# Query rows of the later attentions: written straight into the query buffer, with repeats copied inside it, in place of a round trip through DRAM

## The chip, the cores and the metric

The kernel runs on one core of a Trainium2 chip. Its time is the device time of one execution in microseconds (us). The core has five engines: TensorE (PE, matrix products, with PEld for its weight loads), VectorE (DVE), ScalarE (ACT), GpSimd (POOL) and SyncE (SP), which here does nothing but issue transfers. Sixteen DMA engines move the data; all transfers that SP issues go through one queue (q1 in the profile), those that ACT issues through another (q10).

## The reference

Eight batches of 256 rows with 256 columns go through a chain of eight residual blocks: an attention with 16 heads, a choice of one expert out of eight, a masked attention with 16 heads, a small coupling network, a linear attention, a top-2 mixture with low-rank experts, an attention with one head, and a gated feed-forward block. The change concerns the two 16-head attentions:

```python
q = proj(Q, W_Q, b_Q)                      # (B, 16 heads, 256, 16)
k = proj(K, W_K, b_K)
scores = jnp.einsum('bhqd,bhkd->bhqk', q, k) / jnp.sqrt(jnp.float32(D_K))
attn = jax.nn.softmax(scores, axis=-1)     # the second one: masked first
out = jnp.einsum('bhqk,bhkd->bhqd', attn, v)
x = x + _L0_xattn_ref(_layernorm(x, axis=-1), ctx_1024, ctx_1024, ...)
```

## The kernel before

**Attentions.** There are 16 of them, `(b, m)` with batch `b` and `m` 0 or 1, in the order (0,0), (1,0), (0,1), (2,0), (1,1), (3,0), (2,1) and so on to (7,0), (6,1), (7,1). The scores are formed in bf16, but from numbers that were split into three bf16 parts each, so that the product is as good as one in float32. A head has 16 dimensions, and six products of parts are summed in one matmul over 96 rows: the query buffer `QA[m]` has six blocks of 16 partitions, block `i` being rows 16i to 16i+15, and on each row 16 heads x 256 positions (8 KB). Blocks 0, 1 and 2 hold part 0 of the query, blocks 3 and 4 part 1, block 5 part 2. The key buffer `KA[m]` has the partner parts in its blocks. Two more rows of `QA[m]`, 96 and 97, hold the negative row maximum in two bf16 parts.

**How a query gets there.** A projection on PE leaves the query with (dimension, head) on the partitions; ACT and POOL split it into `qparts[m]` (128 partitions x 2 halves x 3 parts x 256). `QA[m]` wants the dimension alone on the partitions, and the heads along the row. Before the change the two halves of `qparts[m]` are written to a DRAM tensor, `scratch` (line 466, two transfers of 192 KB), and when both have landed, read back block by block (line 499, six transfers of 128 KB). The keys take the same way (lines 466 and 481) and go on doing so. Only the very first attention (0,0) is fed straight from `qparts[0]` and `kparts`: 12 transfers of 64 KB for each of the two, issued by SP (line 521) and ACT (line 785).

**Two passes over the scores.** `heads(b, m)` (line 1586) forms all scores once, so that DVE can take the maximum of each row. For each group of four heads PE turns the maxima (line 1653), ACT copies them into `negm` (line 843), and SP sends them into rows 96 and 97 of `QA[m]`: two transfers of 2 KB a group (line 559). Then the scores are formed once more, transposed and with the maximum subtracted by these two rows (line 1674); the first matmul of each group waits for its two transfers (`m_rows`). From there they go to ACT for the exponential (line 855), back to PE for the sum over values (line 1696), and so on.

**What sets the order.** Every engine runs its instructions strictly in the order in which the program was written. Six threads (`p` preparation, `s` scores, `v` the second pass and what follows, `a`, `b`, `c` the later blocks) are interleaved by one string of letters for each engine, `TURNS`; a letter lets that thread go on to its next `yield`. SP's queue is therefore one list in which the transfers of all threads stand, and a wait in it holds back everything behind it:

```python
def weave(engine, prep, score, value, net, rest, last, early=iter(()), late=iter(())):
    threads = {"p": prep, "s": score, "v": value, "a": net, "b": rest, "c": last, "w": early, "z": late}
    for who in TURNS[engine]:
        next(threads[who], None)
```

Queries of `m` = 0 are fed by the thread `p`, a batch or more ahead of their use; those of `m` = 1 by the thread `s`, one attention ahead. PE's list also holds matmuls on a blank tile, at the beginning and at the end (line 1967).

Of the kernel before, what the change touches and what calls it, by code (L numbers as in the profile page):

```python
# [16 lines left out]
KT = D // P  # L17
H, HD = 16, 16
GH = 4
ITEMS = H // GH  # L20
PARTS = 6

GROUPS = [(0, 3), (1, 2), (2, 1)]
# [110 lines left out]
PLACE = {bm: q for q, bm in enumerate(ATTENTIONS)}  # L134
# [40 lines left out]
def program(nc, x_in, ctx_in, mask_in, pack, nomask, ipack, scratch, out):  # L175
    ctx = ExitStack()
    with ctx:
# [5 lines left out]
        def sem(name, n=0):  # L183
            s = ctx.enter_context(nc.semaphore(name))
            per[s.name] = n
            return s

        def nth(s, r, n):
            return r * per[s.name] + n
# [36 lines left out]
        qparts = [sb(f"qparts{m}", [P, KT, 3, S], BF16) for m in range(2)]  # L226
        KA = [sb(f"KA{m}", [KM, H, S], BF16) for m in range(2)]
        QA = [sb(f"QA{m}", [KM, H, S], BF16) for m in range(2)]
# [88 lines left out]
        for who, steps in LAST.items():  # L317
            done = 0
            for i, name in enumerate(steps):
                n = steps[:i + 1].count(name)  # L320
# [35 lines left out]
        k_ps, v_ps, q_ps = ([sem(f"{n}{m}", 1) for m in range(2)] for n in ("k_ps", "v_ps", "q_ps"))  # L356
        k_f, q_f, v_s = ([sem(f"{n}{m}", 1) for m in range(2)] for n in ("k_f", "q_f", "v_s"))
        k_split, q_split = ([sem(f"{n}{m}", 1) for m in range(2)] for n in ("k_split", "q_split"))
        k_out, q_out = ([sem(f"{n}{m}", 16 * KT) for m in range(2)] for n in ("k_out", "q_out"))
        k_rows = [sem(f"k_rows{m}", 16 * len(GROUPS)) for m in range(2)]  # L360
        q_rows = [sem(f"q_rows{m}", 16 * PARTS) for m in range(2)]
        q_part, q_first, k_first = sem("q_part"), sem("q_first"), sem("k_first")
        third_pe, third_act, third_dve = sem("third_pe", 5), sem("third_act", 3), sem("third_dve", 4)
        xb0_s, xe_s, xb1_s = sem("xb0", 1), sem("xe", 1), sem("xb1", 1)
# [4 lines left out]
        st_ps, exp_s = sem("st_ps"), sem("exp_s")  # L369
# [39 lines left out]
        for name, n in (("sc", E + E * R), ("tw", E * R), ("r1", E), ("r2", E), ("r3", E), ("pick2", E),  # L409
# [9 lines left out]
            s={**{name: last_did[who] for name, who in WHO.items()}, "m_in_s": last_mask_in}, **small_at)  # L419
# [13 lines left out]
        def q_cut(eng, m, b):  # L433
            if (m, b) == (0, 0):
                eng.wait_ge(q_part, 3)
            else:
                eng.wait_ge(q_split[m], nth(q_split[m], b - (m == 0), 1))

        def q_sent(eng, m, b):
            if (m, b) == (0, 0):  # L440
                eng.wait_ge(q_first, 16 * KT * PARTS)
            else:
                eng.wait_ge(q_out[m], nth(q_out[m], b - (m == 0), 16 * KT))

        def q_landed(eng, m, b):
            if (m, b) == (0, 0):
                eng.wait_ge(q_first, 16 * KT * PARTS)
            else:
                eng.wait_ge(q_rows[m], nth(q_rows[m], b - (m == 0), 16 * PARTS))

        block = ctx.enter_context(nc.Block())

# [4 lines left out]
        def _(sp):  # L457
# [6 lines left out]
            def write(parts, which, m, out_s):  # L464
                for k in range(KT):
                    sp.dma_start(scratch[m, which, :, k * P:(k + 1) * P, :].rearrange("c p s -> p c s"),
                                 parts[:, k, :, :]).then_inc(out_s[m], 16)
# [16 lines left out]
                    yield  # L484

            def queries(b, m):
                if b:
                    q_landed(sp, m, b - 1)
                q_cut(sp, m, b)
                write(qparts[m], 0, m, q_out)  # L490
                yield
                q_sent(sp, m, b)
                if b:
                    sp.wait_ge(st_ps, (PLACE[b - 1, m] + 1) * H)
                at = 0
                for part, n in GROUPS:
                    src = scratch[m, 0, part].rearrange("(d h) s -> d (h s)", h=H)
                    for i in range(at, at + n):
                        sp.dma_start(QA[m][i * HD:(i + 1) * HD, :, :].rearrange("p h s -> p (h s)"), src
                                     ).then_inc(q_rows[m], 16)  # L500
                        if i % 2:
                            yield
                    at += n

            def next_cin(b):
                if b < B:
# [1563 lines left out]
```

## Time and profile before

| what | value |
|---|---|
| median of 3 runs | 1091.88 us (1087.68 to 1097.86) |
| the profiled execution, its own time | 1095.82 us |
| its span, first to last instruction | 1094.0 us |
| PE, DVE, ACT, POOL busy | 94%, 59%, 47%, 20% |
| mean granted TensorE clock | 0.975 of full speed |
| DMA: bytes moved, mean rate | 57.07 MB, 52 GB/s |

The profile is that of one execution. Busy time is the union of an engine's instructions; the span is what lies between the first and the last of them, and 1.8 us of the execution's own time lie outside it.

### The profile page before, as it was taken

What the parts mean: (1) busy time and instruction counts of PE and PEld (TensorE: products, weight loads), DVE (VectorE), ACT (ScalarE), POOL (GpSimd) and SP (SyncE); (2) the same over time, 40 slices, a digit from 0 to 9 for tenths busy, and PEclk for the clock granted to TensorE, in tenths of its full rate; (3) what the DMA queues carried; (4) which work ended last, traced back from release to release, by engine and by line L of the source; (5) the groups of instructions that cost most, each with busy time, mean ns of one, the idle gap of its engine ahead of it and who ended that gap; (6) DMA issues with size and microseconds to landing.
All of it is one profiled execution on the core that took longest, in us unless ns stands there. A gap on an engine that the chain in (4) does not pass through costs nothing.

```text
span 1094.0 us, 17887 instructions
## 1 busy us (share of the span) xinstructions
PE 1027.3 (94%) x6322; PEld 700.0 (64%) x6322; DVE 646.5 (59%) x2246; ACT 510.1 (47%) x1091; POOL 220.6 (20%) x314
## 2 busy tenths in 40 slices
PE   7699999888999999999999999999999999999988
PEld 5365664555567765767576756776666756667767
DVE  4245673657667565666667565766667555535553
ACT  1050543465247542574247533574366343765311
POOL 2021330214030220313030222213121112001200
PEclk9599999989999999999999999999999999999999
DMA  7426630324022220403121230412041003000000
GB/s 230 47 52 185 174 83 6 63 45 88 21 47 52 53 46 20 97 10 78 30 57 42 54 63 2 98 43 56 1 86 27 11 7 75 4 10 1 1 10 11
DMA packets 43175, 57.07 MB, mean 52 GB/s; under 512 B 4488, under 2 KB 39056, under 8 KB 39568
## 3 DMA queue, kind: packets, MB, share of 16 engines
q1 hardware_dynamic: 40880, 47.16, 20.1%
q10 hardware_dynamic: 2208, 8.78, 2.6%
q8 instruction: 51, 0.84, 0.3%
q14 instruction: 36, 0.29, 0.1%
HBM read 40.19 MB, written 13.89 MB: 49 GB/s over the span
## 4 chain that ended last, share of the span: by engine, by line
PE 79%; ACT 7%; DMA 4%; DVE 4%; issue 3%; SPq 1%; POOL 1%; ACTq 0%; DVEq 0%
PE bank L1614 11%; PE bank L1947 7%; PE bank L1465 6%; PE bank L1474 6%; PE bank L1674 5%; PE bank L1696 5%; PE bank L1958 4%; PE bank L1731 4%; PE bank L1586 4%; PE bank L1967 3%; DMA QA<-negm 2%; PE bank L1725 2%; PE bank L1677 2%; PE bank L1483 2%; PE bank L1908 1%
## 5 line engine op out<-in xcount | busy, mean ns | idle before, releaser
L855 ACT ACTIVATE PT<-bank 128x512 f32<-128x512 f32 x256 | 153.0, 598 | 194.4 <-PE bank L1677 131.2
L1614 PE MATMUL bank<-w,xhT 128*128 128x512 f32 x256 | 129.0, 610 | 0.0
L1674 PE MATMUL bank<-QA,KA 98*128 98x256 bf16 x512 | 116.1, 280 | 10.7 <-ACT PT L855 7.4
L1153 DVE CUSTOM_DVE_ANT_0 bank<-bank,maskb 128x256 f32<-128x256 f32 x256 | 102.3, 451 | 33.5 <-PE bank L1586 33.1
L1146 DVE TENSOR_REDUCE mx<-bank 128x2 f32<-128x512 f32 x128 | 83.7, 683 | 39.8 <-PE bank L1586 39.3
L1586 PE MATMUL bank<-KA,QA 96*128 96x256 bf16 x512 | 90.9, 279 | 12.6 <-DMA QA<-qparts 8.9
L1198 DVE SCALAR_TENSOR_TENSOR x<-bank,one,x 128x256 f32<-128x256 f32 x128 | 61.8, 483 | 61.1 <-PE bank L1614 58.4
L1947 PE MATMUL bank<-xhBT,wi 128*128 128x256 f32 x336 | 86.7, 391 | 5.2 <-DVE hT L1450 5.1
L1674 PEld LDWEIGHTS bank<-QA,KA 98*128 98x128 bf16 x512 | 46.0, 100 | 68.0 <-ACT PT L855 36.9
L1696 PE MATMUL bank<-PT,vaug 128*32 128x256 f32 x1024 | 72.7, 393 | 3.0 <-ACT PT L855 3.0
L1586 PEld LDWEIGHTS bank<-KA,QA 96*128 96x128 bf16 x512 | 45.7, 100 | 39.3 <-issue 14.8
L1947 PEld LDWEIGHTS bank<-xhBT,wi 128*128 128x128 f32 x336 | 59.8, 192 | 16.9 <-DVE hT L1450 7.4
L1967 PE MATMUL bank<-blank 128*128 128x256 bf16 x440 | 66.8, 289 | 1.2 <-POOL blank L715 1.1
L1677 PE MATMUL bank<-maskb,identb 128*128 128x256 bf16 x256 | 64.9, 277 | 0.0
L1614 PEld LDWEIGHTS bank<-w,xhT 128*128 128x128 f32 x256 | 42.7, 193 | 26.7 <-issue 22.3
L1967 PEld LDWEIGHTS bank<-blank 128*128 128x128 bf16 x440 | 43.6, 103 | 13.4 <-issue 4.8
L1731 PE MATMUL bank<-xhAT,w 128*128 128x256 f32 (+1 forms) x216 | 49.8, 364 | 1.6 <-ACT xhAT L887 1.2
L622 POOL TENSOR_TENSOR kparts<-kf,kparts 128x512 bf16<-128x512 f32 x16 | 18.5, 1157 | 159.3 <-ACT kf L747 159.3
L855 ACT ACT_TABLE_LOAD x36 | 46.2, 1283 | 0.6
L1696 PEld LDWEIGHTS bank<-PT,vaug 128*32 128x32 f32 x1024 | 32.4, 110 | 19.0 <-ACT PT L855 5.9
L695 POOL TENSOR_TENSOR veps_b<-mv_b,epsm 128x2 f32<-128x2 f32 x21 | 4.1, 195 | 197.7 <-DVE mv_b L1333 197.7
L1958 PE MATMUL bank<-wi,hT 128*128 128x256 f32 x168 | 42.4, 385 | 0.0
(310 smaller groups left out, 2013.0 us busy)
## 6 DMA issues: line engine op xcount, KB each, us to landing
QA<-scratch SPq DMA_DIRECT2D x90, 128.0 KB, 4.3
scratch<-kparts SPq DMA_DIRECT2D x30, 192.0 KB, 2.3
KA<-scratch SPq DMA_DIRECT2D x15, 384.0 KB, 4.5
scratch<-qparts SPq DMA_DIRECT2D x30, 192.0 KB, 2.3
KA<-scratch SPq DMA_DIRECT2D x15, 256.0 KB, 5.2
wi<-ipack ACTq DMA_DIRECT2D x1, 2304.0 KB, 8.5
w<-pack ACTq DMA_DIRECT2D x1, 2169.0 KB, 14.5
xin<-x_in SPq DMA_DIRECT2D x8, 256.0 KB, 3.2
```

Source lines behind the costliest of these rows:

```text
L855: act.activation(PT[:, n % RING, :, :].rearrange("p t s -> p (t s)"), st_bank[:, :], ACT.Exp).then_inc(exp_s, 1)
L1146: dve.tensor_reduce(mx[:, i % 4, n % GH, :], s_bank[n % 2][:, :].rearrange("p (t s) -> p t s", t=T), AX.X, ALU.max).then_inc(max_s, 1)
L1153: last = dve.tensor_tensor_reduce(s, s, maskb[:, t, :], op0=ALU.add, op1=ALU.max, scale=1.0, scalar=-HUGE, accum_out=mx[:, i % 4, n % GH, ...
L1586: last = pe.matmul(s_bank[n % 2][:, t * S:(t + 1) * S], QA[m][0:KR, u, t * P:(t + 1) * P], KA[m][0:KR, u, :], start=True, stop=True)
L1614: last = pe.matmul(bank[n % 2][:, :], xhT[:, kk, t * P:(t + 1) * P], W("exp0", KT)[:, kk, i * 512:(i + 1) * 512], start=(kk == 0), stop=(k ...
L1674: last = pe.matmul(st_bank[:, t * S:(t + 1) * S], KA[m][0:KM, v, t * P:(t + 1) * P], QA[m][0:KM, v, :], start=True, stop=(m == 0))
L1677: last = pe.matmul(st_bank[:, t * S:(t + 1) * S], identb[:, :], maskb[:, t, :], start=False, stop=True)
L1696: last = pe.matmul(pv_bank[32 * h:32 * h + 32, 0:S], vaug[m][:, t, g * GH + h, :], PT[:, (i * GH + h) % RING, t, :], start=(t == 0), stop= ...
L1731: last = pe.matmul(ps[:, k * S + lo * P:k * S + hi * P], W(name, KT)[:, kk, k * P:(k + 1) * P], src[:, kk, lo * P:hi * P], start=(kk == 0) ...
L1947: last = pe.matmul(ps[:, i * S + lo * P:i * S + hi * P], ww[:, kk, k * P:(k + 1) * P], L.xhBT[:, kk, lo * P:hi * P], start=(kk == 0), stop ...
L1958: last = pe.matmul(ps[:, t * D:(t + 1) * D], hid[:, kk, t * P:(t + 1) * P], wd[:, kk, :], start=(kk == 0), stop=(kk == HT - 1))
L1967: pe.matmul(ps[:, 0:S], blank[:, 0:P], blank[:, :], start=True, stop=True)
```

## The change

The queries of every attention after (0,0) no longer pass through `scratch`. When the query is split and the buffer is free, SP sends each of the three parts once, straight from `qparts[m]` into blocks 0, 3 and 5 of `QA[m]`: two transfers of 64 KB a part, six in all, each into 8 partitions, with a semaphore `q_once`. When all six have landed, three transfers of 128 KB inside `QA[m]` copy block 0 to blocks 1 and 2 and block 3 to block 4 (`q_rows`). ACT's wait before it overwrites `qparts[m]` is now for `q_once`, and the first matmul of `heads` waits for both semaphores. The number of `yield`s is the same, so the turns of every engine fall as before. The wait for the last second-pass matmul of the attention that used the buffer before (`st_ps`) now stands ahead of the first transfers, and the wait for the old `q_rows` ahead of them is gone.

```diff
--- before.py
+++ after.py
@@ -356,9 +356,10 @@
         k_ps, v_ps, q_ps = ([sem(f"{n}{m}", 1) for m in range(2)] for n in ("k_ps", "v_ps", "q_ps"))
         k_f, q_f, v_s = ([sem(f"{n}{m}", 1) for m in range(2)] for n in ("k_f", "q_f", "v_s"))
         k_split, q_split = ([sem(f"{n}{m}", 1) for m in range(2)] for n in ("k_split", "q_split"))
-        k_out, q_out = ([sem(f"{n}{m}", 16 * KT) for m in range(2)] for n in ("k_out", "q_out"))
+        k_out = [sem(f"k_out{m}", 16 * KT) for m in range(2)]
+        q_once = [sem(f"q_once{m}", 16 * KT * 3) for m in range(2)]
         k_rows = [sem(f"k_rows{m}", 16 * len(GROUPS)) for m in range(2)]
-        q_rows = [sem(f"q_rows{m}", 16 * PARTS) for m in range(2)]
+        q_rows = [sem(f"q_rows{m}", 16 * 3) for m in range(2)]
         q_part, q_first, k_first = sem("q_part"), sem("q_first"), sem("k_first")
         third_pe, third_act, third_dve = sem("third_pe", 5), sem("third_act", 3), sem("third_dve", 4)
         xb0_s, xe_s, xb1_s = sem("xb0", 1), sem("xe", 1), sem("xb1", 1)
@@ -440,13 +441,14 @@
             if (m, b) == (0, 0):
                 eng.wait_ge(q_first, 16 * KT * PARTS)
             else:
-                eng.wait_ge(q_out[m], nth(q_out[m], b - (m == 0), 16 * KT))
+                eng.wait_ge(q_once[m], nth(q_once[m], b - (m == 0), 16 * KT * 3))
 
         def q_landed(eng, m, b):
             if (m, b) == (0, 0):
                 eng.wait_ge(q_first, 16 * KT * PARTS)
             else:
-                eng.wait_ge(q_rows[m], nth(q_rows[m], b - (m == 0), 16 * PARTS))
+                eng.wait_ge(q_once[m], nth(q_once[m], b - (m == 0), 16 * KT * 3))
+                eng.wait_ge(q_rows[m], nth(q_rows[m], b - (m == 0), 16 * 3))
 
         block = ctx.enter_context(nc.Block())
 
@@ -484,23 +486,19 @@
                     yield
 
             def queries(b, m):
-                if b:
-                    q_landed(sp, m, b - 1)
                 q_cut(sp, m, b)
-                write(qparts[m], 0, m, q_out)
-                yield
-                q_sent(sp, m, b)
                 if b:
                     sp.wait_ge(st_ps, (PLACE[b - 1, m] + 1) * H)
-                at = 0
-                for part, n in GROUPS:
-                    src = scratch[m, 0, part].rearrange("(d h) s -> d (h s)", h=H)
-                    for i in range(at, at + n):
-                        sp.dma_start(QA[m][i * HD:(i + 1) * HD, :, :].rearrange("p h s -> p (h s)"), src
-                                     ).then_inc(q_rows[m], 16)
-                        if i % 2:
-                            yield
-                    at += n
+                for part, i in ((0, 0), (1, 3), (2, 5)):
+                    for k in range(KT):
+                        sp.dma_start(QA[m][i * HD + k * 8:i * HD + (k + 1) * 8, :, :].rearrange("d h s -> d (h s)"),
+                                     qparts[m][:, k, part, :]).then_inc(q_once[m], 16)
+                yield
+                q_sent(sp, m, b)
+                for src, i in ((0, 1), (0, 2), (3, 4)):
+                    sp.dma_start(QA[m][i * HD:(i + 1) * HD, :, :].rearrange("p h s -> p (h s)"),
+                                 QA[m][src * HD:(src + 1) * HD, :, :].rearrange("p h s -> p (h s)")).then_inc(q_rows[m], 16)
+                    yield
 
             def next_cin(b):
                 if b < B:
```

SP's list in the steady part, where the queries of (b, 0) are fed while (b-1, 1) is in its second pass (so the maxima go to `QA1`). Before:

```order
L466 DMA scratch<-qparts0 128x3x256 [waits q_split0,q_rows0]
L466 DMA scratch<-qparts0 128x3x256
L559 DMA QA1<-negm 1x4x256 [waits negm_s]
L559 DMA QA1<-negm 1x4x256
L499 DMA QA0<-scratch 16x4096 [waits st_ps,q_out0]
L499 DMA QA0<-scratch 16x4096 x5
L559 DMA QA1<-negm 1x4x256 [waits negm_s]
```

The same place in SP's list with the change:

```order
L494 DMA QA0<-qparts0 8x16x256 [waits st_ps,q_split0]
L494 DMA QA0<-qparts0 8x16x256 x5
L557 DMA QA1<-negm 1x4x256 [waits negm_s]
L557 DMA QA1<-negm 1x4x256
L499 DMA QA0<-QA0 16x4096 [waits q_once0]
L499 DMA QA0<-QA0 16x4096 x2
L557 DMA QA1<-negm 1x4x256 [waits negm_s]
```

Ahead of the first pair of maxima stand six transfers where two stood, and ahead of the second pair three where six stood, behind another wait.

SP's list where the queries of (b, 1) are fed just before the first maxima of (b+1, 0) are due (these go to `QA0`). Before:

```order
L466 DMA scratch<-qparts1 128x3x256 [waits q_split1,q_rows1]
L466 DMA scratch<-qparts1 128x3x256
L499 DMA QA1<-scratch 16x4096 [waits st_ps,q_out1]
L499 DMA QA1<-scratch 16x4096 x3
L559 DMA QA0<-negm 1x4x256 [waits negm_s]
L559 DMA QA0<-negm 1x4x256
L499 DMA QA1<-scratch 16x4096 x2
```

The same place in SP's list with the change:

```order
L494 DMA QA1<-qparts1 8x16x256 [waits st_ps,q_split1]
L494 DMA QA1<-qparts1 8x16x256 x5
L499 DMA QA1<-QA1 16x4096 [waits q_once1]
L499 DMA QA1<-QA1 16x4096
L557 DMA QA0<-negm 1x4x256 [waits negm_s]
L557 DMA QA0<-negm 1x4x256
L499 DMA QA1<-QA1 16x4096
```

Here the pair of maxima stands behind eight transfers and the wait for `q_once1`, where it stood behind six and the wait for `q_out1`. On the other engines no instruction has moved.

## Rows read from the trace of the kernel before

**Rows 1.** The page: chain that ended last, shares of the span by engine.

```profile
PE 79%; ACT 7%; DMA 4%; DVE 4%; issue 3%; SPq 1%; POOL 1%; ACTq 0%; DVEq 0%
```

**Rows 2.** Busy time by stretch: stretch, us, then each engine; PEclk, DMA share, GB/s.

```profile
167.20:170.40 3.20, 3.14 (x9) 1.55 (x10) 0.12 (x1) 0.60 (x1) 0.00 (x0) 0.50 0.02 5
500.00:620.00 120.00, 116.92 (x719) 79.23 (x719) 76.59 (x272) 62.47 (x130) 27.24 (x37) 1.00 0.22 49
```

**Rows 3.** What PE waited for from 140 to 860 us: total, times, longest.

```profile
PE bank L1674 <- DMA QA<-negm: 2.5, 6, 1.2
```

**Rows 4.** The page, transfers by line: count, KB of each, median us to landing.

```profile
QA<-scratch SPq DMA_DIRECT2D x90, 128.0 KB, 4.3
...
scratch<-qparts SPq DMA_DIRECT2D x30, 192.0 KB, 2.3
```

**Rows 5.** Lines 499 and 521 alone: ns that SP takes to issue one; landing for line 499.

```profile
L499 SPq DMA_DIRECT2D QA<-scratch x90: 315/420/1629, 83.5 to 911.4; - x90
...
DMA to landing us min/median/max: 2.8/4.3/9.5
...
L521 SPq DMA_DIRECT2D QA<-qparts x12: 609/710/2088, 23.4 to 33.6; - x12
```

**Rows 6.** Busy time by stretch: straight copies at the start; scratch write, then block reads.

```profile
20.00:22.00 2.00, 2.00 (x21) 1.79 (x20) 0.00 (x0) 0.00 (x0) 2.00 (x3) 1.00 0.44 89
41.00:43.00 2.00, 0.00 (x0) 0.00 (x0) 0.00 (x0) 0.00 (x0) 0.00 (x0) 0.50 0.64 60
...
443.00:444.00 1.00, 1.00 (x8) 0.81 (x7) 0.96 (x5) 0.08 (x1) 0.00 (x0) 1.00 0.84 265
...
447.00:448.00 1.00, 1.00 (x10) 0.86 (x9) 0.22 (x1) 0.29 (x3) 1.00 (x2) 1.00 1.07 131
```

**Rows 7.** SP in order of time, 441 to 457 us: start, us, line.

```profile
441.61 0.90 SPq L466 DMA_DIRECT2D scratch<-qparts  x2
444.36 1.71 SPq L499 DMA_DIRECT2D QA<-scratch  x4
446.75 1.22 SPq L559 DMA_DIRECT2D QA<-negm  x2
448.02 1.02 SPq L499 DMA_DIRECT2D QA<-scratch  x2
```

**Rows 8.** The chain that ended last, 441 to 457 us: start, us, what.

```profile
447.40 3.75 DMA QA<-negm
...
451.19 0.39 PE bank L1674 x2
```

**Rows 9.** SP in order of time, 388.5 to 405 us.

```profile
389.48 0.91 SPq L466 DMA_DIRECT2D scratch<-qparts  x2
391.60 1.20 SPq L559 DMA_DIRECT2D QA<-negm  x2
```

**Rows 10.** PE in order of time, 388.5 to 405 us.

```profile
396.40 0.37 PE L1674 MATMUL bank<-QA,KA 98*128 98x256 bf16 x1
```

**Rows 11.** The chain that ended last, 262.5 to 272 us.

```profile
262.80 0.38 SPq L466
...
264.38 1.61 DMA QA<-negm
...
266.04 0.28 PE bank L1674
...
268.72 0.35 ACT negm L843
...
269.71 4.01 DMA QA<-negm
```

**Rows 12.** The last attention (7,1): SP, then PE, in order of time.

```profile
905.51 0.91 SPq L466 DMA_DIRECT2D scratch<-qparts  x2
908.27 4.25 SPq L499 DMA_DIRECT2D QA<-scratch  x6
...
917.26 0.60 PE L1586 MATMUL bank<-KA,QA 96*128 96x256 bf16 x4
```

More of the change, by code:

```diff
@@ L486, in queries @@
             def queries(b, m):
+                q_cut(sp, m, b)
                 if b:
-                    q_landed(sp, m, b - 1)
-                q_cut(sp, m, b)
-                write(qparts[m], 0, m, q_out)
+                    sp.wait_ge(st_ps, (PLACE[b - 1, m] + 1) * H)
+                for part, i in ((0, 0), (1, 3), (2, 5)):
+                    for k in range(KT):
+                        sp.dma_start(QA[m][i * HD + k * 8:i * HD + (k + 1) * 8, :, :].rearrange("d h s -> d (h s)"),
+                                     qparts[m][:, k, part, :]).then_inc(q_once[m], 16)
                 yield
                 q_sent(sp, m, b)
-                if b:
-                    sp.wait_ge(st_ps, (PLACE[b - 1, m] + 1) * H)
-                at = 0
-                for part, n in GROUPS:
-                    src = scratch[m, 0, part].rearrange("(d h) s -> d (h s)", h=H)
-                    for i in range(at, at + n):
-                        sp.dma_start(QA[m][i * HD:(i + 1) * HD, :, :].rearrange("p h s -> p (h s)"), src
-                                     ).then_inc(q_rows[m], 16)
-                        if i % 2:
-                            yield
-                    at += n
+                for src, i in ((0, 1), (0, 2), (3, 4)):
+                    sp.dma_start(QA[m][i * HD:(i + 1) * HD, :, :].rearrange("p h s -> p (h s)"),
+                                 QA[m][src * HD:(src + 1) * HD, :, :].rearrange("p h s -> p (h s)")).then_inc(q_rows[m], 16)
+                    yield
             def next_cin(b):
```

## The prediction

> **What bounds the kernel now.** First the chain that ended last, by engine: PE holds 79% of the span, and no other engine more than 7% [rows 1]. Then busy time by stretch: in the steady part, where one batch takes some 122 us, PE is busy 116.92 us of 120 [rows 2], so it stands still for 3 us a batch, and whatever makes it stand still longer goes nearly whole into the time. Its list is in one fixed order; it cannot go round a wait. So the question is which transfers PE waits for. The list of PE's waits names only one in the steady part: the first second-pass matmul of a group (line 1674) waits for the row maxima, `QA<-negm`, 2.5 us in 6 times [rows 3]. That sum is small, but the transfer stands on the chain with far more than the idle time: 3.75 us at 447.40 [rows 8], 1.61 and 4.01 us at 264.38 and 269.71 [rows 11]. It is 2 KB; it takes that long only because SP's list and queue put it behind the query blocks. The copy of the query itself is never waited for after the start: it lands well ahead of its `heads`, with one close case, the last [rows 12]. I therefore read the change by one thing: what it does to the maxima that stand behind the queries in SP's list. There are 15 such places ("visits"), one for each attention after (0,0).
>
> **Removed.** Two writes of 192 KB into the scratch, 2.3 us to land [rows 4], moving 265 GB/s [rows 6], and six block reads of 128 KB at 131 GB/s [rows 6], 1.0 us each when queued, with 0.42 us of SP each [rows 5]. None of it is waited for by itself; what it costs is the place it takes ahead of the maxima.
>
> **Added: six straight transfers of 64 KB.** The trace has twelve of the same shape, for (0,0), line 521. SP needs 0.71 us for one, against 0.45 for a scratch write (0.90 for two) [rows 5, 7]: six take 4.3 us of SP where the writes took 0.9. Their rate is the disputed number. At 20 to 22 us, where the issue set the pace, the same shape moved 89 GB/s; from 41 to 43 us, with a backlog, 60 GB/s with the DMA engines busy 0.64 and nothing else going on [rows 6]. The scratch write, with the same 512-byte pieces from the same tile, moved 265. So it is the destination, 8 partitions, that is slow: reads into 16 partitions moved 131 [rows 6], about twice as much. The bounds are: as fast as SP issues (4.3 us), or 60 GB/s. I take 60, since six are a backlog: 6 x 65.5 KB / 60 GB/s = 6.6 us. To that comes what the scratch write needs beyond its transfer, 2.3 - 197 KB / 265 GB/s = 1.5 us. The six have landed 8.1 us after the first issue, where the scratch write let SP go on 2.75 us after it (441.61 to 444.36) [rows 7].
>
> The Trainium skill ("SBUF — State Buffer", "Door 1: The DMA port swizzle") has a rule that speaks against this change: DMA bandwidth goes by how many of 16 ports the partitions reach, some 27 GB/s each. By its table 8 partitions in a row reach two ports, 54 GB/s, and 16 reach four, 109; the trace shows 60 and 131, in the same proportion. With 54 the six would take 7.3 us instead of 6.6, and the sum below would be 9 us higher.
>
> **Added: three copies inside `QA`.** No row shows one. The block reads write the same 16 partitions, 1.0 us each when queued, 2.8 us at least to land [rows 5, 6]. I take that, as the destination is the same. From below: without DRAM at the source, perhaps half a us less to land. From above: reading 16 partitions as slowly as 8 are written, 2.2 us each.
>
> **Visits where the maxima stand right behind the six** (all of m = 0 after (1,0), and those of (0,1) and (1,1): eight). At 389.48 SP issues until 393.8, where the maxima went out at 391.60 [rows 9]; they now lie behind the six in the queue and land at 389.5 + 8.1, PE goes on 0.3 us later, at 397.9. It used them at 396.40 [rows 10]: 1.5 us late. At 262.80 the same gives 271.2 against 266.04, 5.2 late; but the next pair then waits behind no copies. It was ready at 269.07 and took 4.6 us in all; ready at 274.3 it takes 0.6 + 1.6 (the unhindered landing at 264.38) and lands at 276.5 against 273.7, so 2.8 us of the 5.2 are left [rows 11]. The same arithmetic over the eight, from 116.26 to 753.93, gives 0.3, 2.5, 3.0, 2.8, 1.5, 1.8, 1.4 and 0: 13.3 us.
>
> **Visits where the maxima stand behind copies too** ((2,1), (3,1), (4,1), (5,1) behind two, (6,1) behind three). At 441.61: the six have landed at 449.7, where SP now waits with the maxima (ready since 446.75) behind it. Two copies 0.84, the pair 1.2 [rows 5, 7]; the first copy lands at 449.7 + 2.8 = 452.5, the second at 453.5, the maxima at 453.7. Before: 451.15 [rows 8]. 2.6 us late, on the chain. Four of these 10.4 us, (6,1) 1.7: 12.1 us.
>
> **The last one**, (7,1): the copies land at 905.51 + 8.1 + 2.8 + 2.0 = 918.4, PE wanted them at 917.26 [rows 12]: 1.3 us. The first, (1,0), is fed long before its use: nothing.
>
> **Edits with no cost.** `st_ps` ahead of the first transfer: its matmuls had ended before every visit, so SP does not wait there. ACT's wait for `q_once`: a batch old. PE's second wait: the same landing.
>
> **Sum.** 13.3 + 12.1 + 1.3 = 26.7 us of PE standing still. Not all of it stays: PE idles 3 us a batch anyway, and a stall lets ACT and DVE get ahead, so that some of that idle time goes. I take 0.8: 21 us. Against that, stalls cost clock. Right after the longest wait for maxima (1.2 us) the granted clock was 0.50 from 167.2 to 170.4 us, that is 1.2 GHz where 2.4 GHz is full [rows 2, 3]; 3.2 us at half speed cost up to 1.6 us. Fourteen new stalls might bring none, or one each (24 us); I take three, 5 us. So +26 us: the profiled execution would go from 1095.8 (span 1094.0) to 1122, and the median of the three runs, 1091.88, to **1118 us**, 2.4% slower. A measurement of this kernel can tell about 1% from no change.
>
> **The rivals.**
>
> *The straight transfers run at the pace of SP.* For it: 89 GB/s at 20 us [rows 6]; against it: the long stretch at 60. Six would land after about 6 us. The places behind copies come out even (441.61 + 6.1, copies and pair issued by 449.8, landed at 451), the places behind the six lose about 1 us each on average: +5 us, 1097 us, no change that can be told. This is the case that isn't slower. Chance 0.15.
>
> *Faster.* If SP also issued a straight transfer in 0.45 us, as it does a scratch write, the six would land after 4.5 us and the maxima at 441.61 would come 1.9 us sooner than now, since two copies stand ahead of them and not four. It decides at an issue below 0.55 us and a rate above 110 GB/s together. Five such visits and the pairs behind six copies give -12 us, 1080 us. Every one of the twelve issues took 0.609 us or more [rows 5]: 0.03.
>
> *Copies inside `QA` are slow.* At 2.2 us each the five visits behind copies lose 2.3 to 3.4 us more, and the second pairs of the early visits also: +16 before the factor, in all 39 us, 1131 us. No row excludes it: 0.14.
>
> *The clock goes with most stalls.* Ten dips and more: +38 us, 1130 to 1138 us: 0.08.
>
> **How the numbers follow.** The forecast has 0.60, with a range of its own from 1105 to 1128 (factor 0.5 to 1, none to five dips, 54 or 60 GB/s). The range that should hold 8 in 10 takes in the nearer half of the fast case and the slow copies: 1098 to 1134. Slower by over 1% (above 1103): 0.60 + 0.14 + 0.08 = 0.82; within 1%: 0.15; faster: 0.03.
>
> **What would show it.** In the list of waits, PE at the second-pass matmul for `QA<-negm` should grow from 2.5 us to over 20 in the same stretch. SP should wait for `QA<-qparts` 3 to 4 us at every visit. With one of the six in the queue behind another, the rate should be 60 GB/s. The copies should land one us apart. If the six land within 6 us, or PE's waits don't grow, the forecast is wrong; if the waits grow and the time doesn't, the factor is.

## The result: 5.2% slower, and the profile after

The changed kernel takes **1146.88 us** (median of four runs, 1145.75 to 1148.35) against 1093.22 us (1087.68 to 1097.86) for the kernel before: ratio 1.052, 95% interval 1.047 to 1.057. The forecast of 1118 had the direction and the place right, and about half of the size; the time is outside the range of 1098 to 1134. (A repetition, e0 below, gives the same; one of its four executions ran in a slower state of the chip, 1157.98 us at a clock of 0.945, and is left out.)

The pages: busy time before the change, then busy time and the chain that ended last by engine with it:

```profile
PE 1027.3 (94%) x6322; PEld 700.0 (64%) x6322; DVE 646.5 (59%) x2246; ACT 510.1 (47%) x1091; POOL 220.6 (20%) x314
```

```profile
PE 1047.0 (92%) x6322; PEld 711.0 (62%) x6322; DVE 646.8 (57%) x2246; ACT 510.7 (45%) x1091; POOL 220.4 (19%) x314
...
PE 67%; ACT 8%; DMA 7%; SPq 6%; POOL 4%; DVE 4%; issue 3%; ACTq 0%; DVEq 0%
```

Against [rows 1], SP's own issuing (SPq) went from 1% of the chain to 6% and DMA from 4% to 7%. PE does the same 6322 matmuls as before in 1047.0 us instead of 1027.3. The span is 1143.9 us instead of 1094.0. That closes the account: **+49.9 us is +30.2 us of PE idle (96.9 for 66.7) and +19.7 us of PE being busy longer with the same work.** The start hides a part of it. Counted from PE's first matmul of the first attention's `heads` (at 45.90 us before, 39.17 with the change), the rest takes 1048.1 and 1104.7 us for the same 6182 matmuls: +56.6 us, 33.9 of them idle and 22.7 busy.

What PE waited for (total, times, longest), from 140 to 900 us, the same places as in [rows 3], and then over the whole run:

```profile
PE bank L1672 <- DMA QA<-negm: 34.8, 11, 5.6
...
PE bank L1672 <- DMA QA<-negm: 36.1, 12, 5.6
...
PE bank L1584 <- DMA QA<-qparts: 4.2, 1, 4.2
```

The wait for the maxima went from 2.5 us in 6 to 34.8 us in 11; over the whole run it was 2.8, so it grew by 33.3. The last line is the start, where the kernel before waited 8.9 us; it happened to give 4.7 us back; e0, the same kernel again, doesn't wait there at all.

The two new lines of SP alone (ns to issue one: least, median, most), and what line 499's copies took to land and made wait:

```profile
L494 SPq DMA_DIRECT2D QA<-qparts x90: 608/609/1655, 70.7 to 960.1; - x90
...
L499 SPq DMA_DIRECT2D QA<-QA x45: 524/584/1726, 82.1 to 964.7; - x45
...
  PE bank L1584: 1.4, 1
...
DMA to landing us min/median/max: 3.3/3.8/12.7
```

The visit that answers to [rows 7, 8] (the one at 441.61 before), first SP in order of time, then the chain:

```profile
462.76 3.98 SPq L494 DMA_DIRECT2D QA<-qparts  x6
471.30 1.22 SPq L499 DMA_DIRECT2D QA<-QA  x2
472.56 1.69 SPq L557 DMA_DIRECT2D QA<-negm  x2
```

```profile
466.13 5.15 DMA QA<-qparts
...
471.30 0.59 SPq L499
...
471.93 0.58 SPq L499
...
472.56 0.66 SPq L557
...
473.26 2.64 DMA QA<-negm
...
475.94 0.39 PE bank L1672 x2
```

This is the cause at the five visits where the maxima stand behind copies, in six lines. SP issues six transfers until 466.7, then waits at its next instruction until they have landed, at 471.3; 8.5 us have gone by in which SP could send nothing else. Two copies follow, and only then the maxima, which had been ready since 467.9. They leave at 472.6 and land at 475.9.

At the eight visits where the maxima stand right behind the six, SP doesn't wait for a landing ahead of them. There they lose the 4 us of the six issues, and then are long in flight, since the six are still under way. The chain at the visit that answers to [rows 11], and at the same place in e4, where the six land faster:

```profile
271.57 3.99 DMA QA<-negm
```

```profile
266.68 1.68 DMA QA<-negm
```

PE in order of time at this visit and at the one before it in the text, with the wait ahead of the matmul in brackets:

```profile
275.61 0.39 PE L1672 MATMUL bank<-QA,KA 98*128 98x256 bf16 x1 [5.56 <-DMA QA<-negm]
...
475.94 0.39 PE L1672 MATMUL bank<-QA,KA 98*128 98x256 bf16 x2 [3.84 <-DMA QA<-negm]
```

Busy time by stretch, with PEclk, DMA share and GB/s at the end, as in [rows 2, 6]: the six in flight, the copies in flight, and the stretches at half clock by the two waits above:

```profile
466.00:467.00 1.00, 1.00 (x9) 0.92 (x8) 0.85 (x4) 1.00 (x4) 0.45 (x1) 1.00 0.63 62
472.00:473.00 1.00, 0.10 (x1) 0.00 (x0) 0.42 (x1) 0.84 (x2) 0.00 (x0) 1.00 1.06 123
476.40:483.00 6.60, 6.60 (x23) 4.59 (x21) 3.10 (x9) 1.32 (x4) 0.00 (x0) 0.50 0.33 102
271.50:281.60 10.10, 5.99 (x31) 2.54 (x32) 2.28 (x10) 1.90 (x4) 1.82 (x3) 0.50 0.41 53
```

The six move 62 GB/s, the copies 123, about as forecast. What was not forecast is the third and fourth row: with a standstill of 3.84 us the granted clock is at 0.50 (1.2 GHz) for the next 6.6 us, and around the one of 5.56 us for over 10 us, in 5.99 of which PE works. Half of the working time is lost: up to 3.3 and 3.0 us. Mean clock of the run, kernel before and changed kernel:

```profile
core 0: 1094.0 us, clock 0.975
```

```profile
core 0: 1143.9 us, clock 0.952
```

If all that is missing is time at 0.50, then 2 x (1 - clock) x span is the time spent at 1.2 GHz: 55 us before, 110 us after. Half of the 55 us more is lost work, up to 27 us, less where a part of it falls into a standstill; 19.7 showed.

### The profile page after: what moved, and what is told of

Its sections match the earlier page's. It is cut to its first block, busy times and chain, and to the rows that moved or that the text cites. A ratio compares the mean times of both kernels' runs of the same rounds, so it can differ in the third digit from the quotient of the medians.

```text
span 1143.9 us, 17895 instructions
## 1 busy us (share of the span) xinstructions
PE 1047.0 (92%) x6322; PEld 711.0 (62%) x6322; DVE 646.8 (57%) x2246; ACT 510.7 (45%) x1091; POOL 220.4 (19%) x314
## 4 chain that ended last, share of the span: by engine, by line
PE 67%; ACT 8%; DMA 7%; SPq 6%; POOL 4%; DVE 4%; issue 3%; ACTq 0%; DVEq 0%
PE bank L1612 10%; PE bank L1945 6%; PE bank L1672 5%; PE bank L1694 5%; PE bank L1463 4%; PE bank L1472 4%; SPq L494 4%; PE bank L1956 4%; DMA QA<-qparts 3%; DMA QA<-negm 3%; PE bank L1729 3%; PE bank L1584 3%; PE bank L1965 3%; PE bank L1675 2%; PE bank L1481 2%
## 5 line engine op out<-in xcount | busy, mean ns | idle before, releaser
L1672 PE MATMUL bank<-QA,KA 98*128 98x256 bf16 x512 | 119.9, 288 | 43.7 <-DMA QA<-negm 36.1
L1584 PE MATMUL bank<-KA,QA 96*128 96x256 bf16 x512 | 94.2, 288 | 8.7 <-DMA QA<-qparts 4.2
L1694 PEld LDWEIGHTS bank<-PT,vaug 128*32 128x32 f32 x1024 | 32.7, 111 | 18.8 <-ACT PT L853 5.5
```

Source lines behind the costliest of these rows:

```text
L1584: last = pe.matmul(s_bank[n % 2][:, t * S:(t + 1) * S], QA[m][0:KR, u, t * P:(t + 1) * P], KA[m][0:KR, u, :], start=True, stop=True)
L1672: last = pe.matmul(st_bank[:, t * S:(t + 1) * S], KA[m][0:KM, v, t * P:(t + 1) * P], QA[m][0:KM, v, :], start=True, stop=(m == 0))
L1694: last = pe.matmul(pv_bank[32 * h:32 * h + 32, 0:S], vaug[m][:, t, g * GH + h, :], PT[:, (i * GH + h) % RING, t, :], start=(t == 0), stop= ...
```

## The experiments

All twelve runs together. "Maxima" is PE's wait for `QA<-negm`; "idle" is span less PE busy; "at 1.2 GHz" is worked out as above. "Behind the start" is the span from PE's first matmul of the first attention's `heads` on. Those four are from the one profiled execution, the time is the median of the timed runs, and the ratio is against the kernel before on the same chip.

| run | us | ratio (95%) | maxima | idle | at 1.2 GHz | behind the start |
|---|---|---|---|---|---|---|
| kernel before | 1093.22 | | 2.8 | 67 | 55 | 1048 |
| changed kernel | 1146.88 | 1.052 (1.047, 1.057) | 36.1 | 97 | 110 | 1105 |
| e0, changed again | 1141.87 | 1.050 (1.042, 1.058) | 37.7 | 95 | 98 | 1104 |
| e1, maxima first | 1153.74 | 1.055 (1.047, 1.064) | 44.5 | 113 | 109 | 1112 |
| e2, scratch once | 1131.75 | 1.033 (1.025, 1.042) | 22.8 | 82 | 72 | 1084 |
| e3, PE given blank work | 1132.64 | 1.035 (1.027, 1.043) | 9.3 | 67 | 45 | 1086 |
| e4, rows apart | 1100.30 | 1.010 (1.006, 1.013) | 7.5 | 65 | 75 | 1065 |
| e7, order changed | 1113.51 | 1.022 (1.017, 1.027) | 8.2 | 82 | 58 | 1065 |
| e8, rows apart and order | 1080.89 | 0.993 (0.990, 0.996) | none listed | 59 | 35 | 1044 |
| e5, before with rows apart | 1080.12 | 0.993 (0.989, 0.997) | 0.6 | 55 | 45 | 1042 |
| e13, e5 again | 1081.62 | 0.989 (0.985, 0.993) | 0.9 | 57 | 30 | 1040 |
| e9, e5 with the order | 1092.32 | 0.999 (0.995, 1.002) | 4.3 | 65 | 50 | 1055 |
| e11, before, SP held | 1177.23 | 1.077 (1.071, 1.082) | 57.5 | 126 | 140 | 1137 |
| e12, ACT sends the maxima | 1134.27 | 1.039 (1.033, 1.045) | 11.3 | 100 | 85 | 1099 |

The start needs care. PE waits there for the queries of (0,0), which only the runs with rows apart feed differently: 8.8 to 9.7 us in the profiled executions of the kernel before, e1, e7, e11 and e12, 4.2 in that of the changed kernel, and nothing in the others, e0 among them. The first `heads` start at 44.9 to 45.9 us in the first group and at 34.6 to 36.2 in the last. So spans and idle times of single executions differ by some 10 us for this alone (that of e2 lay 11 us and that of e3 9 us under its median, that of e12 11 us above); the last column is free of it.

### e1: the maxima ahead of the six

The theory was that the maxima are late because they stand behind the six transfers. At 13 visits the next pair of maxima is moved ahead of them in SP's list.

```diff
+def maxima_first(turns):
+    at = {t: [i for i, c in enumerate(turns) if c == t] for t in "ps"}
+    visits = [at["p"][15 + 14 * (b - 2) + 8] for b in range(2, B)] + [at["s"][4 * b] for b in range(B - 1)]
...
+        turns[i:j + 1] = ["v"] + turns[i:j]
...
+TURNS["sync"] = maxima_first(TURNS["sync"])
```

> The changed kernel with one edit in SP's list: at 13 of the 15 visits the pair of maxima that stood next behind the six straight transfers goes ahead of them. Theory A (PE's standstill comes from maxima that stand behind the straight transfers in SP's list and in the queue, and all of the loss, the clock dips too, follows from that): PE's waits for QA<-negm fall from 36 us to under 8, the half-speed time after the start falls from about 90 us to about 30, and the time goes back to 1092 to 1105 us. Theory B (the straight transfers cost something by themselves, by contention with PE's reads of QA, or the queries come too late): the waits move to the heads (line 1584) or PE is slower everywhere, and the time stays above 1130 us.

It cured nothing: 1153.74 us, and the wait for maxima grew to 44.5 us. SP in order of time, and PE behind it:

```profile
479.94 1.22 SPq L571 DMA_DIRECT2D QA<-negm  x2
481.26 3.98 SPq L508 DMA_DIRECT2D QA<-qparts  x6
489.77 1.86 SPq L513 DMA_DIRECT2D QA<-QA  x3
491.67 1.16 SPq L596 DMA_DIRECT2D xhB<-ctx_in  x1
492.94 1.07 SPq L482 DMA_DIRECT2D scratch<-kparts  x2
494.05 1.32 SPq L571 DMA_DIRECT2D QA<-negm  x2
```

```profile
497.41 0.61 PE L1686 MATMUL bank<-QA,KA 98*128 98x256 bf16 x2 [5.25 <-DMA QA<-negm]
```

The pair moved ahead is in time; the **next** pair, ready at 488.5, now lies behind the landing, three copies and two further jobs, and PE stands 5.25 us for it. So the six transfers are not an obstacle for one pair: from the first of them to the landing SP's list is closed for 8.5 us, and whichever pair falls due meanwhile is late.

### e2: half of the change

One write to the scratch, three block reads, and the three repeats copied inside `QA`. This tells the straight transfers apart from the copies.

```diff
+                write(qparts[m], 0, m, q_out)
+                yield
+                sp.wait_ge(q_out[m], nth(q_out[m], b - (m == 0), 16 * KT))
...
-                    for k in range(KT):
-                        sp.dma_start(QA[m][i * HD + k * 8:i * HD + (k + 1) * 8, :, :].rearrange("d h s -> d (h s)"),
-                                     qparts[m][:, k, part, :]).then_inc(q_once[m], 16)
+                    src = scratch[m, 0, part].rearrange("(d h) s -> d (h s)", h=H)
+                    sp.dma_start(QA[m][i * HD:(i + 1) * HD, :, :].rearrange("p h s -> p (h s)"), src
+                                 ).then_inc(q_once[m], 16)
```

> Half of the change: the parts still go through the scratch (two writes, then three block reads of 128 KB), and only the three repeats are copied inside QA, behind a wait for the reads. Theory A: where the maxima stand right behind the write (8 visits) nothing is lost, where they stand behind the copies (5 visits) SP waits about as long as in the changed kernel (2.7 us for the write, then about 5 for the reads), so that PE's waits for the maxima are about half of the changed kernel's, 12 to 20 us, and the time is 1110 to 1125 us. Theory C (the 8-partition destinations alone are the trouble): as fast as before, 1092 us.

SP in order of time at the same visit:

```profile
446.28 0.91 SPq L469 DMA_DIRECT2D scratch<-qparts  x2
449.04 1.26 SPq L498 DMA_DIRECT2D QA<-scratch  x3
453.87 1.20 SPq L503 DMA_DIRECT2D QA<-QA  x2
455.11 1.71 SPq L563 DMA_DIRECT2D QA<-negm  x2
```

1131.75 us and 22.8 us of waits for maxima, both somewhat above what was expected (1110 to 1125, 12 to 20): 3.3% of the 5.2% are already there without one straight transfer. This form has two waits for landings ahead of the copies instead of one, and closes SP's list for 7.6 us (446.28 to 453.87), not much less than the 8.5 of the changed kernel. How its 3.3% divide between the second wait and the copies was not taken apart.

### e3: what the clock costs

The changed kernel, with 257 matmuls on a blank tile put ahead of eleven of the twelve waits, so that PE is busy while it waits. They add work and take no wait away.

```diff
+FILL = {(0, 1, 0): 26, (2, 0, 0): 24, (1, 1, 1): 42, (3, 0, 0): 32, (2, 1, 2): 8, (4, 0, 0): 28, (3, 1, 2): 14,
+        (5, 0, 0): 28, (4, 1, 2): 11, (6, 0, 0): 26, (7, 0, 0): 18}
...
+                            if n % GH == 0:
+                                for _ in range(FILL.get((b, m, n // GH % ITEMS), 0)):
+                                    pe.matmul(st_bank[:, 0:S], blank[:, 0:P], blank[:, :], start=True, stop=True)
```

> The changed kernel with 257 matmuls on the blank tile on PE, put ahead of eleven of its waits for maxima (8 to 42 each, as many as fit the standstill of the profiled execution); nothing else is changed. Theory A2 (about half of the loss is clock: PE stands still, the granted clock falls to half, and 60 us more at half speed cost up to 30 us): the dips vanish for the most part, and the time falls by 15 to 28 us to 1120 to 1132 us, although PE has more to do. Theory D (the dips cost little, the loss is the waits and what follows from them): the time stays within 5 us of 1147 or rises.

The kernel with more work is faster than the changed kernel: 1132.64 us, ratio 1.035 against 1.052, just above the expected 1120 to 1132. Blank work by its group, the wait that is left, and the mean clock:

```profile
L1673 PE MATMUL bank<-blank 128*128 128x256 bf16 x257 | 32.0, 284 | 0.0
...
PE bank L1676 <- DMA QA<-negm: 9.3, 10, 2.9
...
core 0: 1121.5 us, clock 0.980
```

PE's busy time is 1054.5 us with 32.0 of blanks in it, so 1022.5 for the kernel's own matmuls: as before the change (1027.3), and 24.5 less than in the changed kernel. The span fell by 22.4 us, behind the start by 18.8, the median by 14.2 and the ratio by 1.7 points. The clock's share of the loss is thus shown by itself: **about 20 us of the 50 come from running at 1.2 GHz behind the standstills**, and the other 30 are the standstills.

### e4: rows apart

The destination is what the forecast held slow: 8 partitions in a row for the straight transfers, 16 for the copies. In e4 row d of part i lies in partition 6d + i instead of 16i + d, in `QA` and in `KA` (whose reads become six). The same bytes go to every sixth partition, those of the first attention too.

```diff
-                        sp.dma_start(QA[m][i * HD + k * 8:i * HD + (k + 1) * 8, :, :].rearrange("d h s -> d (h s)"),
+                        sp.dma_start(QA[m][k * 8 * PARTS + i:(k + 1) * 8 * PARTS:PARTS, :, :].rearrange("d h s -> d (h s)"),
                                      qparts[m][:, k, part, :]).then_inc(q_once[m], 16)
...
-                    sp.dma_start(QA[m][i * HD:(i + 1) * HD, :, :].rearrange("p h s -> p (h s)"),
-                                 QA[m][src * HD:(src + 1) * HD, :, :].rearrange("p h s -> p (h s)")).then_inc(q_rows[m], 16)
+                    sp.dma_start(QA[m][i:KR:PARTS, :, :].rearrange("p h s -> p (h s)"),
+                                 QA[m][src:KR:PARTS, :, :].rearrange("p h s -> p (h s)")).then_inc(q_rows[m], 16)
```

> The changed kernel with the rows of QA and KA in another order: row 6d+i instead of 16i+d, so that a block lies on every sixth partition and not on 16 in a row (keys then take six block reads of 128 KB and not three larger ones). If the straight transfers are slow because 8 neighbouring partitions share few ports into SBUF, they now run at the pace of SP, 100 GB/s or more, the six land about 6 us after the first issue and the three copies in half a us each: the time falls to 1105 to 1125 us. If what limits them is the number of partitions, or anything in the source, they stay at 60 GB/s and the time stays near 1147 us.

1100.3 us, under the 1105 to 1125 that I expected: 1.0% above the kernel before instead of 5.2%. A part of that helps any version: against e5 below, the kernel before with its rows apart (0.993), 1.7% are left. Of the page, the transfers by line (count, KB each, median us to landing), and SP at the same visit:

```profile
QA<-QA SPq DMA_DIRECT2D x45, 128.0 KB, 2.3
...
445.50 3.97 SPq L495 DMA_DIRECT2D QA<-qparts  x6
451.17 1.21 SPq L500 DMA_DIRECT2D QA<-QA  x2
```

The six have landed 5.7 us after the first issue instead of 8.5, 1.7 us after the last; the issue (3.97 us) now sets their pace. The copies land in 2.3 us instead of 3.8. For these transfers nothing but the partitions was changed. The Trainium skill ("SBUF — State Buffer", "Door 1: The DMA port swizzle") has a rule that fits: neighbouring partitions share ports, so that 8 or 16 in a row reach few of 16 ports, while every sixth partition, by its table of ports, reaches more. The trace agrees with its proportion (62 and 123 GB/s for 8 and 16 in a row), and the measured rates stand above its figures, 109 for 16 and, as an estimate from its 27.2 GB/s a port, 54 for 8.

### e7 and e8: the order of SP's list

Here SP's list has, at the same 13 visits: a pair of maxima, the six, whatever else stands there, the **next** pair, and only then the wait for the landing and the copies. So SP no longer waits at a place where a pair is due.

```diff
+        turns[i:end] = ["v", turns[i]] + between + ["v"] + [turns[i]] * 3 + after
...
+TURNS["sync"] = maxima_between(TURNS["sync"])
```

> The changed kernel with SP's list in the order: a pair of maxima, the six straight transfers, the next pair, and only then the wait for the six and the three copies inside QA, at 13 visits. Putting one pair ahead (e1) only moved the wait to the next pair, which comes 6 to 9 us later, while a visit holds SP for 10 us. Theory A (what costs is the time for which the list is closed to maxima, 4 us of issue and 4 to 5 us of waiting for the landing): here it is closed for no more than 4 us at a time and never for the landing, PE's waits for QA<-negm fall under 8 us, the half-speed time to about 30 to 40 us, and the time is 1090 to 1105 us. Theory B (the transfers cost by themselves, in the queue or in SBUF): above 1125 us.

1113.51 us, above the 1090 to 1105 that I expected. The wait for the maxima did go (8.2 us), at the price of another:

```profile
PE bank L1602 <- DMA KA<-scratch: 8.6, 3, 4.3
PE bank L1690 <- DMA QA<-negm: 8.2, 7, 1.8
```

The keys of the next attention, which stand behind the copies, are now late: 8.6 us of a wait that the changed kernel does not list. e8 has this order and the rows apart:

> Both cures on the changed kernel, rows on every sixth partition and the order of e7: no wait for maxima longer than 1 us, 1078 to 1092 us; by the theory that the round trip through the scratch was a cost of its own it would be faster than e5, by the theory that it was hidden anyway the two are equal within 1%.

1080.89 us, 0.993. The same 90 straight transfers and 45 copies through the same queue, and PE waits for no maxima at all. So neither their number nor their bytes cost anything by themselves; what transfers do that land late, beyond closing the list, e8 can't say (see e12).

### e5, e13 and e9: the kernel before, with rows apart

Is the removed round trip worth anything? e5 has it, with the rows apart (and, like e4 and e8, six key reads in place of three).

```diff
-                        sp.dma_start(QA[m][i * HD:(i + 1) * HD, :, :].rearrange("p h s -> p (h s)"), src
+                        sp.dma_start(QA[m][i:KR:PARTS, :, :].rearrange("p h s -> p (h s)"), src
```

> The kernel before with the rows of QA and KA in another order, a block on every sixth partition: the block reads of 128 KB should take about half a us each and not one when queued, so that maxima behind them land about 2 us sooner at 5 visits and on the chain. Theory of the ports: 1076 to 1088 us, 0 to 1.5% under before. Against it stand three more issues of SP at every key visit (6 in place of 3, 1.3 us).

```profile
QA<-scratch SPq DMA_DIRECT2D x90, 128.0 KB, 2.6
```

The block reads land in 2.6 us instead of 4.3 [rows 4], and the time is 1080.12 us, 0.7% under the kernel before. e8, without the round trip, is at 1080.89 on the same chip: **the best version without the round trip is no faster than the best one with it.** The two differ in SP's order as well, and the order decides: in the old one the version without the round trip is 1.7% slower (e4 1.010, e5 0.993), in that of e7 0.6% faster (e8 0.993, e9 0.999, on different chips). e13 repeats e5 with other runs:

> The kernel before with rows apart once more, for a firmer number on the fastest version: 0.5 to 1.1% under the kernel before.

1081.62 us, 0.989: 0.7 to 1.1% under the kernel before, and with e8, from which no run tells it apart, the fastest version. In the profiled execution of e5 only 5.8 us of the 16.0 won lie behind the start; how much of the gain is the faster landing of the block reads and how much the start isn't settled. e9 gives e5 the order of e7:

> The kernel before with its rows apart (e5) and with SP's list in the order of e7: maxima, write of the parts, maxima, block reads. With rows apart no wait for maxima was left over 1 us, so the order has nothing to give: 1076 to 1084 us, equal to e5 and e8 within 1%.

It is not equal to e5, as I had expected, but gives nearly all of its gain back (0.999 against the kernel before). The maxima wait is 4.3 us and the one for keys 4.5: an order that suits one form of the visit does not suit the other.

### e11: SP held, nothing else

The kernel before, whole, and at each visit 13 transfers of 16 bytes from an input to an output that nobody reads, 7 behind the scratch write and 6 behind its landing. They use no partition of `QA` and carry no load worth the name; they only occupy SP.

```diff
+            def hold(b, m, lo, hi):
+                for i in range(lo, hi):
+                    at = ((b + B * m) * 13 + i) * 4
+                    sp.dma_start(unread[:, at:at + 4], mask_in[0:1, 0:4]).then_inc(held, 16)
```

> The kernel before, round trip and all, with 13 transfers of 16 bytes from DRAM to DRAM, which nobody reads, in SP's list at each of the 15 visits: 7 behind the write of the parts and 6 behind the wait for it, some 5.5 us of SP in all. They carry no load worth the name and touch no SBUF. Theory A (what cost was the time for which SP's list was closed to the maxima, whatever closed it, and the clock that PE's standstill took with it): PE waits for QA<-negm 20 us or more, over 60 us at half speed after the start, 1115 to 1145 us. Theory B (the load of the straight transfers on the queue and on the ports of SBUF): within 1% of the kernel before.

```profile
484.22 0.90 SPq L468 DMA_DIRECT2D scratch<-qparts  x2
485.16 7.88 SPq L491 DMA_DIRECT2D unread<-mask_in  x13
493.08 1.83 SPq L508 DMA_DIRECT2D QA<-scratch  x4
494.95 1.25 SPq L568 DMA_DIRECT2D QA<-negm  x2
...
L491 SPq DMA_DIRECT2D unread<-mask_in x195: 558/559/1467, 78.6 to 996.8; - x195
```

1177.23 us, 7.7% slower, with 57.5 us of waits for maxima. SP was held for longer than I had meant (7.88 us and not 5.5, since an issue of 16 bytes takes 0.56 us, hardly less than one of 64 KB), so the size is above the expected 1115 to 1145 and says little; the kind says what matters: **SP's list being closed is enough** to make the maxima late, without a byte more into the slow partitions.

### e12: another engine sends the maxima

If it is SP's list, then maxima that are not in it should be in time. In the changed kernel ACT issues them itself, right behind its own copy.

```diff
-                        sp.wait_ge(negm_s, i + 1)
-                        for c in range(2):
-                            sp.dma_start(QA[m][KR + c:KR + c + 1, g * GH:(g + 1) * GH, :],
...
+                act.wait_ge(negm_s, i + 1)
...
+                    act.dma_start(QA[m][KR + c:KR + c + 1, g * GH:(g + 1) * GH, :],
+                                  negm[c * GH:(c + 1) * GH, i % 2, :]).then_inc(m_rows[i % 2], 16)
```

> The changed kernel with the maxima taken off SP's list: ACT, which makes them, issues their two transfers itself, into its own queue; the queries go as in the change, straight and slow. ACT pays 1.2 us for each of 64 groups, 77 us in all, of which it has 600 us idle, but at the start of an attention the exponentials come later for it. If the closed list is the cause, PE's waits for QA<-negm fall from 36 to under 12 us although the straight transfers are as slow as ever, and the time is 1095 to 1120 us; if the load of the straight transfers holds up the maxima in any queue, the waits stay above 25 us and the time above 1135 us.

```profile
PE bank L1673 <- ACT PT L854: 21.9, 33, 1.8
PE bank L1673 <- DMA QA<-negm: 11.3, 8, 3.0
...
282.72 4.07 SPq L494 DMA_DIRECT2D QA<-qparts  x6
284.44 1.21 ACTq L841 DMA_DIRECT2D QA<-negm  x2
...
285.06 4.75 DMA QA<-negm
```

The wait for maxima fell from 36 to 11.3 us, as the theory said. At the five visits behind copies it is gone. Nearly all of the rest, 10.9 us, lies at the visits right behind the six, where it was 18.4: the last lines show why. The maxima leave ACT while the six are under way and take 4.75 us to land, 3.9 to 5.3 at the other visits of this kind, though they are in another queue. So SP's closed list isn't the whole cause: **slow transfers in flight also hold up the maxima of another queue.** What they share that is slow, these runs don't show; in e4, with the six landing faster, the pair at the same place took 1.68 us.

But the time, 1134.27 us, is above the expected 1095 to 1120, behind the start only 5.9 us less than in the changed kernel: each pair now holds ACT for 1.2 us, and PE waits for ACT's exponentials 21.9 us in 33 times (7.4 in 17 before the change, 7.2 in 16 after it). A good part of the cost was moved, not removed.

## Why the prediction was right in direction and too small

**Right, as the runs showed.** PE's list is the bound, and the copy of the query isn't what it waits for: behind the start the only wait for it is 1.4 us at (7,1), forecast 1.3 (the terms given for it add up to 1.15). The maxima behind the queries are the price; e11 and e12 show it from two sides. SP waited for `QA<-qparts` as said, 51.9 us at 15 visits. The straight transfers move at 60 to 62 GB/s, slow by their destination (e4). The edits held free (`st_ps`, `q_once`, the removed round trip) show no cost and no gain: e8, which has them, is equal to e5. Of the sum's parts, the eight visits behind the six came to 18.4 us of waits (13.3 forecast as lateness), the five behind copies to 17.8 (12.1).

**The term of the clock failed most.** "Fourteen new stalls might bring none, or one each (24 us); I take three, 5 us." It was 19.7 us (PE's busy time), and e3, which filled the waits and nothing else, gave 18.8 us back behind the start. Both factors were off. The number of dips: I had one row, behind a wait of 1.2 us, and took it as a chance event; the waits of 3 to 5 us that I forecast myself were longer than anything behind the start in the trace of before, and at those two that I show the clock was down. And the length: I took 3.2 us each, and these lasted 6.6 and 10.1 us, up to 3.3 and 3.0 us of work lost. The rival that named this ("ten dips and more", 0.08) should have been the forecast, and its 1130 to 1138 would still have been low.

**The factor of 0.8 failed.** "PE idles 3 us a batch anyway, and a stall lets ACT and DVE get ahead, so that some of that idle time goes." None did: waits for maxima +33.3, (7,1) +1.4, less 4.7 at the start, is +30.0 us, and the idle time grew by 30.2 (behind the start +33.9, for +34.7 of waits). The old idle is made of short waits of other kinds (`PT` 7.4 and now 7.2 us, `hT` 5.1 and 5.3, `vaug` 3.6 and 3.6), and these are still in the list at the same sizes.

**The waits were sized short: 26.7 us for 34.7.** Two things make it up. The first is a mistake in the mechanism. At 262.80 I took the first pair as 5.2 us late and let the second win back nearly half, 2.8 left, because its own landing would be only 2.8 us later than before. But PE comes to the second pair 5.2 us later too, and in the kernel before it stood there for 0.15 us only, so that there was nothing to win back:

```profile
273.77 0.28 PE L1674 MATMUL bank<-QA,KA 98*128 98x256 bf16 x1 [0.15 <-DMA QA<-negm]
```

At the visit that answers to it PE stood 5.56 us at the first pair. It didn't wait at the second, and needed 10.2 us from one to the other (275.61 to 285.80) for what took 7.7 before (266.04 to 273.77): the way between was not shortened but lengthened, at 0.50 of the clock. At the three late visits of this kind the forecast held (1.5, 1.8 and 1.4 us; measured 1.3, 1.9 and 1.5); at the other early ones it was short as well (0.3, 2.5 and 3.0; measured 1.3, 3.5 and 3.3).

The second is the sizes behind copies. The six took 8.5 us and not 8.1; from their landing to that of the maxima it took 4.6 us (471.30 to 475.90) and not 4.0, since the copies moved 123 GB/s, took 3.3 us at least to land and not 2.8, and 0.58 us of SP each instead of 0.42. The four visits forecast at 2.6 us came to 3.5 to 4.2.

By terms: forecast 21 + 5 = 26 us; measured 30 + 20 = 50 us (34 + 23 = 57 behind the start).

**The rivals.** Straight transfers at SP's pace (1097 us): false for the rows in a row, and what e4 comes near to, which then gave 1100.3. Copies inside `QA` at 2.2 us each: no, 1.07. Faster: nowhere near.

**Open.** How e2's 3.3% divide. Why the start waits 9 us in some profiled executions, 4.2 in one and not at all in others, of the same code even (changed kernel and e0): it wasn't tried. What holds up the maxima in ACT's queue in e12. And how the loss divides, at the eight visits, between the six issues ahead of the maxima and their long way behind them: at the one shown, e4 has the issues and a short way, and PE still waits 3.2 us of 5.6.

## What to carry to other kernels

Ask of a transfer not only when it lands but for how long it closes the list of the engine that issues it: the time of the issues, plus every wait for a landing ahead of the next instruction; then look what falls due in that time, and again one item further on. A small transfer sent while large ones crawl into few partitions is late even from another queue (4.75 us here for 2 KB, against 1.68 with rows apart). Price a standstill of the bound engine at its length plus the clock behind it (here some 20 us for 33 us of waits), and take no discount for idle time that has other causes: lateness is won back only where the engine stood idle before. Before a round trip is removed, look whether anybody waits for it; and when a block transfer into few neighbouring partitions is slow, try first to spread its rows over the partitions, which here took 4.2 of the 5.2% off the changed kernel and 0.7 to 1.1% off the kernel before.

## What the runs showed of the hardware that was not expected

- Issuing a transfer cost SP 0.56 us for 16 bytes (195 of them, least 0.558), 0.61 for 64 KB and 0.58 for a copy of 128 KB; a block read of 128 KB cost 0.42 with its rows in a row [rows 5] and 0.59 with them apart (e5). It doesn't go by size.
- Giving PE blank work to do while it waits made the kernel faster than letting it stand still, by 14 us in the median and 18.8 behind the start (e3: mean clock 0.980 against 0.952).
- 2 KB sent by ACT into its own queue took 4.75 us to land while SP's six transfers into 8 partitions each were under way (e12).
- Copies inside SBUF, 16 partitions to 16 others, moved 123 GB/s and landed in 3.8 us at the median; spread over every sixth partition they landed in 2.3 us.
